# Spreading the node half of a third score pass: even batches stay, odd batches run beside the first and the fourth convolution

## What is computed

```python
def _sage_layer(h, edge_src, edge_dst, W, b):
    msg_sum = segment_sum(h[edge_src], edge_dst, num_segments=n)
    deg = segment_sum(ones_like(edge_dst), edge_dst, num_segments=n)
    m = msg_sum / maximum(deg, 1.0)[:, None]
    return relu(concatenate([h, m], axis=1) @ W + b)
...
x = _layernorm(x + _L0_gnn_ref(...))
x = _layernorm(x + _L1_gnn_ref(...))
x = _layernorm(x + _L2_gnn_ref(...))
x = _layernorm(x + _L3_gnn_ref(x, src, dst, W1, b1, W2, b2))
```

## Time and profile before

| | us |
|---|---|
| median of 3 runs | 5108.9 (5107.18 to 5110.88) |
| the profiled execution, its own time | 5106.98 |
| its span, first to last instruction | 5105.2 |
| busy: TensorE 3933.3, DVE 3846.9, ACT 3417.5, POOL 3021.6 | 77%, 75%, 67%, 59% |
| mean granted TensorE clock | 0.906 |

### The profile page before, as it was taken

The page is one execution under the profiler, slowest core; times in us unless marked ns, Lnnn a source line. Parts: engine busy times, 40 slices in busy tenths (PEclk is TensorE's granted clock), DMA queues, the critical chain, the costliest instruction groups (busy, mean ns, idle before and its releaser), DMA issues. The chain is left out here.

```text
span 5105.2 us, 107944 instructions
## 1 busy us (share of the span) xinstructions
PE 3933.3 (77%) x23968; PEld 2888.5 (57%) x23968; DVE 3846.9 (75%) x14905; ACT 3417.5 (67%) x11259; POOL 3021.6 (59%) x2914
## 2 busy tenths in 40 slices
PE   2999999565996798994998995897767676665554
PEld 1666766343775454773555774443666566665544
DVE  4999999676998787887886998898548777444443
ACT  0889999554886576884776885887448788333332
POOL 2888888475552122661223551787767676777777
PEclk9999999788998899997999997998889888997666
DMA  2566666587996576994777994775546566543332
GB/s 61 164 185 197 200 197 192 169 287 245 353 352 235 185 243 200 346 352 146 237 240 237 352 348 174 228 225 173 157 148 208 186 206 191 156 148 116 92 100 70
DMA packets 605098, 1059.41 MB, mean 208 GB/s; under 512 B 109304, under 2 KB 129930, under 8 KB 604924
## 3 DMA queue, kind: packets, MB, share of 16 engines
q1 hardware_dynamic: 523196, 919.04, 52.7%
q0 software_dynamic: 81728, 138.51, 10.7%
HBM read 607.70 MB, written 453.39 MB: 208 GB/s over the span
## 5 line engine op out<-in xcount | busy, mean ns | idle before, releaser
L2403 POOL DMA_INDIRECT got_c<-table,src_row x980 | 932.1, 951 | 373.1 <-issue 295.0
L1399 POOL DMA_INDIRECT src_got_s<-table,src_row x588 | 554.9, 944 | 474.2 <-PE bank L1445 139.8
L2431 PE MATMUL bank<-pick_c,got_c 128*128 128x128 f32 x1960 | 349.4, 334 | 425.3 <-DMA got_c<-table,src_row 355.6
L1997 PE MATMUL bank<-w_all,dt_m 128*128 128x512 f32 x1176 | 568.1, 599 | 35.3 <-DMA dt_m<-delta_t 33.7
L2431 PEld LDWEIGHTS bank<-pick_c,got_c 128*128 128x128 f32 x1960 | 300.9, 235 | 470.7 <-issue 292.1
L1971 POOL TENSOR_TENSOR part_m<-part_m,half_sum_m 128x512 f32<-128x512 f32 x98 | 158.7, 1619 | 586.0 <-DVE half_sum_m L2204 586.0
L1554 ACT ACTIVATE z_s<-z_s,shift_s,dev_s 128x128 f32<-128x128 f32 x1176 | 483.8, 486 | 1.4 <-DVE shift_s L1673 0.9
L2534 ACT COPY agg_c<-bank 128x512 f32<-128x512 f32 x245 | 143.0, 583 | 450.0 <-DVE bank L1835 298.3
L789 PEld LDWEIGHTS bank<-w_mean,ht 128*128 128x128 f32 x2352 | 313.2, 194 | 143.4 <-issue 143.4
L2455 PE MATMUL bank<-w_c,agg_c 128*128 128x128 f32 x1960 | 377.9, 321 | 2.3 <-ACT agg_c L2534 2.2
L1828 DVE COPY tails_c<-tails_c 128x1 f32<-128x1 f32 x245 | 37.0, 151 | 424.9 <-PE bank L2431 419.6
(11 more groups left out here) (331 smaller groups left out, 11840.9 us busy)
## 6 DMA issues: line engine op xcount, KB each, us to landing
table<-rows SPq DMA_DIRECT2D x294, 256.0 KB
x_s<-table SPq DMA_DIRECT2D x294, 256.0 KB
x_c<-table SPq DMA_DIRECT2D x245, 256.0 KB
table<-mid_s SPq DMA_DIRECT2D x196, 256.0 KB
table<-z_s SPq DMA_DIRECT2D x196, 256.0 KB
table<-z_c SPq DMA_DIRECT2D x196, 256.0 KB
own_rows_s<-table SPq DMA_DIRECT2D x147, 256.0 KB
pick_t_s<-picks_t SPq DMA_DIRECT2D x147, 256.0 KB
```

The source lines that it names most:

```text
L1399: nc.gpsimd.indirect_dma_start(out=src_got[r][:, g, :], out_offset=None, in_=tables[l].rows, in_offset=bass.IndirectOffsetOnAxis(ap=src_ro ...
L1997: nc.tensor.matmul(b_h[k % n_h][:, :], dt[b.slot][:, k, :], w_all[:, l, :, :].rearrange("p h d -> p (h d)"), start=True, stop=True).then_i ...
L2403: nc.gpsimd.indirect_dma_start(out=got[r][:, g, :], out_offset=None, in_=t_in.rows, in_offset=bass.IndirectOffsetOnAxis(ap=src_row[:, t:t ...
L2431: ins = nc.tensor.matmul(b_sum[r][:, k * P:(k + 1) * P], got[b.slot][:, k, :], pick[r][:, k, :], start=k == 0, stop=sage, skip_group_check ...
```

## The change

The third score pass is called with a new flag, `solo`. Then a step treats one edge batch and only node batch `2b`. Its lists are new (`step_solo`), and with one node batch a step the two banks and the paired tiles alternate by step. The 49 odd node batches go to `convolve(0, ...)` and `convolve(3, ...)`, 25 to each (one is done twice): every second step of these phases starts one node batch (`even(b)`). Its tiles are few: one bank `b_turn` for all three uses (turned rows, hidden rows, hidden rows turned back), one bank `b_node` for the second product, and one `nxt` and one `nht`. The waits of the new functions are those that these tiles call for. Each of the two phases also loads the node weights and biases by four more transfers at its start, and TensorE waits for them. Their loops run longer at the end, by up to seven counts on ACT.

```diff
+                        def step_solo(at):        # TensorE, third pass
+                            b = at(1)
+                            if b:
+                                hidden(b, 0)
+                            b = at(2)
+                            if b:
+                                turn_delta(b)
+                                product(b, 0)
+                                turn_hidden(b, 0)
+                            b = at(3)
+                            if b:
+                                score(b)
+                            b = at(0)
+                            if b:
+                                turn_rows(b, 0)
+                            b = at(1)
+                            if b:
+                                spread(b)
...
+                        def step_solo(at):        # ACT, third pass
+                            b = at(1)
+                            if b:
+                                relu(b, 0)
+                            b = at(3)
+                            if b:
+                                deviation(b, 0)
+                            b = at(2)
+                            if b:
+                                delta_out(b)
+                            b = at(3)
+                            if b:
+                                normalise(b, 0)
+                            b = at(0)
+                            if b:
+                                turn_out(b, 0)
+                            b = at(3)
+                            if b:
+                                score_out(b)
...
+                        def step_solo(at):        # DVE, third pass
+                            b = at(3)
+                            if b:
+                                scale(b, 0)
+                            b = at(2)
+                            if b:
+                                residual(b, 0)
+                                middle(b, 0)
+                                moments(b, 0)
+                            b = at(1)
+                            if b:
+                                set_bias(b, 0)
+                                difference(b)
...
+                def even(b):                      # the convolutions
+                    return nodes and b and b.slot % 2 == 0
...
+                        def load_nodes(b):        # SP
+                            r = b.slot // 2
+                            hold(sp, nz_read, b.ring(1, -2))
...
+                        def node_turn(b):         # TensorE
+                            pe.wait_ge(nx_in[r], b.ring4(16))
+                            hold(pe, nmid_made, b.ring(1, -1))
+                            for g in range(GB):
+                                ins = nc.tensor.transpose(b_turn[:, g * P:(g + 1) * P], nx[r][:, g, :], ident[:, :])
+                            ins.then_inc(n_turned, 1)
+                        def node_hidden(b):
+                            pe.wait_ge(nxt_made, b.ring(1))
+                            nc.tensor.matmul(b_turn[:, :], nw1[:, :], nxt[:, :], start=True, stop=True).then_inc(nh_made, 1)
+                        def node_middle(b):
+                            pe.wait_ge(nht_made, b.ring(1))
+                            for g in range(GB):
+                                ins = nc.tensor.transpose(b_turn[:, g * P:(g + 1) * P], nht[:, g, :], ident[:, :])
+                            ins.then_inc(nmid_turned, 1)
+                        def node_product(b):
+                            pe.wait_ge(n_bias, b.ring(1))
+                            for g in range(GB):
+                                ins = nc.tensor.matmul(b_node[:, g * D:(g + 1) * D], nht[:, g, :], nw2[:, :],
+                                                       start=False, stop=True, skip_group_check=True)
+                            ins.then_inc(ny_made, 1)
+                        def node_steps(at):
+                            b = at(4)
+                            if even(b):
+                                node_middle(b)
+                            b = at(5)
+                            if even(b):
+                                node_product(b)
+                            b = at(3)
+                            if even(b):
+                                node_hidden(b)
                         def step_gcn_relu(at):
                             b = at(1)
                             if b:
                                 sum_edges(b)
+                            node_steps(at)
                             b = at(2)
                             if b:
                                 product(b)
+                            if even(b):
+                                node_turn(b)
                             b = at(1)
                             if b:
                                 add_own(b)
...
                             b = at(2)             # step_sage_relu
                             if b:
                                 product(b)
+                            node_steps(at)
+                            b = at(2)
+                            if even(b):
+                                node_turn(b)
...
+                        def node_turned(b):       # ACT
+                            act.wait_ge(n_turned, b.ring(1))
+                            nc.scalar.copy(nxt[:, :], b_turn[:, :]).then_inc(nxt_made, 1)
+                        def node_relu(b):
+                            act.wait_ge(nh_made, b.ring(1))
+                            hold(act, ny_made, b.ring(1, -1))
+                            nc.scalar.activation(flat(nht), b_turn[:, :], ACT.Relu, bias=nb1[:, 0:1]).then_inc(nht_made, 1)
+                        def node_middle_out(b):
+                            act.wait_ge(nmid_turned, b.ring(1))
+                            hold(act, nmid_stored[r], b.ring4(16, -16))
+                            nc.scalar.copy(flat(nmid[r]), b_turn[:, :]).then_inc(nmid_made, 1)
+                            hold(act, nz_read, b.ring(1, -1))
+                            nc.scalar.copy(b_node[:, :], nb2[:, :]).then_inc(n_bias, 1)
...
+                        def node_steps(at):
+                            b = at(3)
+                            if even(b):
+                                node_relu(b)
+                            b = at(4)
+                            if even(b):
+                                node_middle_out(b)
+                            b = at(6)
+                            if even(b):
+                                node_deviation(b)
+                            b = at(7)
+                            if even(b):
+                                node_normalise(b)
                         def step_relu(at):
                             b = at(0)
                             if b and not sage:
                                 diagonals(b)
-                            b = at(2 if sage else 1)
-                            if b:
+                            b = at(2)
+                            if b and sage:
                                 set_bias(b)
                                 sums_out(b)
+                            node_steps(at)
+                            b = at(1)
+                            if b and not sage:
+                                set_bias(b)
+                                sums_out(b)
+                            b = at(2)
+                            if even(b):
+                                node_turned(b)
...
-        edge_scores(2, (io["L3_gnn_W1"][0:D, :], io["c_L3_gnn_b1"]), (io["L3_gnn_W2"][0:D, :], io["b_L3_gnn_b2"]), t[6], t[7], t[8])
+        edge_scores(2, (io["L3_gnn_W1"][0:D, :], io["c_L3_gnn_b1"]), (io["L3_gnn_W2"][0:D, :], io["b_L3_gnn_b2"]), t[6], t[7], t[8], True)
```

More of the change, by code:

```diff
@@ L1216, in _, with edge_scores @@
                         skewed(dve, nb, 2, step, 4)
-        def edge_scores(l, first, second, t_in, t_mid, t_out):
+        def edge_scores(l, first, second, t_in, t_mid, t_out, solo=False):
             with ExitStack() as c, Semaphores(nc) as sem:
@@ L1232, in edge_scores @@
                 scores = pairs("scores", (P, P))
-                x, z = ([fours(f"{n}{h}_") for h in range(2)] for n in ("x", "z"))
+                halves = range(1 if solo else 2)
+                x, z = ([fours(f"{n}{h}_") for h in halves] for n in ("x", "z"))
                 xt = pairs("xt")
@@ L2387, in step @@
                                 store(b)
-                        skewed(sp, nb, 6 if norm else 4, step, 4)
+                            b = at(6)
+                            if even(b):
+                                store_node_middle(b)
+                            b = at(9)
+                            if even(b):
+                                store_nodes(b)
+                        skewed(sp, nb, 9 if nodes else 6 if norm else 4, step, 4)
+                        if nodes:
+                            for r in range(2):
+                                sp.wait_ge(nmid_stored[r], 16 * ((n_own + 1 - r) // 2))
```

(22 more changed lines are left out.)

200 lines of the change are left out of this document (147 added, 53 removed).

## The result

The changed kernel takes 5132.93 us (median of five runs), the kernel before 5108.65 us beside it: a ratio of 1.0045, 95% interval 1.0034 to 1.0057, so 0.45% slower. The forecast was 5130 us. One of the five executions, at 7644.67 us, belongs to a slower state and is left out of the ratio; the other four have a median of 5130.8 us. The profiled execution spans 5126.7 us.

What follows compares the result with a forecast made beforehand. The third pass was full on all engines and transfers; POOL's gathers bound the first and fourth convolution. -96 + 14 + 104 = +22 on 5106.98 gives 5129, with 2 for the median 5130 us; range 5104 to 5176 (8 in 10).

Steps and rivals of the forecast that it cites:

- Third pass, -96: Third score pass: one node batch less a step, 5.5 us in place of 7.52, 49 steps; bounds -98 and -76.
- the loop: Third pass: DVE's list, then TensorE's turn_delta and product, in a chain of 5.44 us a step.
- (b): Third pass: the transfers set the pace, step 5.9 us, 5150 us in all; chance 0.12.
- Fourth convolution, +104: Fourth convolution: TensorE and ACT take turns, 6.9 us a step in place of 5.0; bounds 88 and 118.
- +12: Fourth convolution's end: the last node batch follows the last product alone, about 13 us against 1 now.
- +3: Fourth convolution's start: TensorE waits for four more transfers and fills one more bank; bounds 0 and 5 us.
- +83 and +6: Fourth convolution's steps: 44 steps pay 1.9 us each (+83); the five before have 12.3 us for two (+6).
- First convolution, +14: First convolution: POOL still sets the pace, rate 0; tail +12 and start +2; bounds 10 and 35 us.
- +2: First convolution's start: the addition there was put at 2 us.
- released half a step and more ahead of need: SP's queue: its waits, for a result's store and the load held by the residual, end early; no time added.
- (a): Fourth convolution: the node work hides there too, 5042 us in all; chance 0.10.
- (c): Fourth and first convolution: pauses lower TensorE's clock, +31 and +20 us, 5181 us together; chance 0.12.

Runs made afterwards that it cites:

- the two reorderings: Changed kernel, fourth convolution alone: node steps ahead of the product on TensorE (5632.54 us), or normalisation ahead of the relu on ACT (5682.49 us); changed kernel there 5718.13 us.

## Why the prediction was right

**Third pass, -96.** Measured -95.8, at 5.49 us a step against 5.44 for the loop, 5.2 for the transfers and 5.5 as taken. The waits and the steps of 5.41 us speak for the loop, and the DMA share of 0.99 for the transfers; both are within 0.3 us of the step. The number was right, and which of the two sets it is open: with 0.6 us taken out of the loop on other chips, 0.1 to 0.2 us a step was gained. Rival (b), 5.9 us a step, fell.

**Fourth convolution, +104.** Measured +104.1, and its parts are close. The pair of steps took 13.64 us where 13.8 was summed. The last product ends 19.4 us ahead of the next phase (4599.1 to 4618.55) where it ended 4.1 ahead (4593.4 to 4597.48), so the tail costs +15.4 and not +12. Part of that is the lower clock: over 4598 to 4618 us the granted clock is 0.59, and the eight matmuls of a node product take 1.91 us in place of 1.06. From the start of the phase to the first product it is some 14 us in both kernels, so the start costs nothing, not +3. That these two misses cancel is luck. What is left, 104.1 - 15.4 = 88.7, is the loop, for which the terms +83 and +6 stood. That the order is the cause, and not the amount of work, is shown by the two reorderings, on other chips but with the same cost of the phase (103.8 us): -84 and -37 us at equal work. The second is one item of the chain, 34 us by its row, and it comes within 3 us.

**First convolution, +14.** Measured +13.2. POOL kept its 1.25 us a gather. The last product ends 15.9 us ahead of the next phase (3716.6 to 3732.48) in place of 4.4: +11.5 for the tail. The first product comes 15.2 us after the start of the phase in place of 13.7: +1.6 for the start, put at +2. The runs with one batch less took 8.9 us off the tail on another chip.

**A step that failed without a price.** The prediction held that the node load is "released half a step and more ahead of need". The waits of the changed kernel for 3550 to 3700 us say otherwise:

```profile
PEld bank L2599 <- DMA nx_c<-table: 22.7, 15, 1.7
PE bank L2599 <- DMA nx_c<-table: 19.8, 15, 1.5
```

TensorE waits 1.3 us for it in every pair of steps. POOL's 10.0 us a pair hid this in the first convolution, ACT's chain hid it in the fourth, and it came out when that chain was cut.

**The rivals.** (a), that the node work hides in the fourth convolution, fell on the order of the lists; with `node_hidden` ahead most of it does hide. (c), the clock, fell too: TensorE waits 3.3 us for the sums in each pair of steps (0.84 and 2.46 in the timeline), and the granted clock in that stretch is 1.00. In the first convolution it rose from 0.86 to 1.00, with TensorE's busy share up from 73% to 85%. On a slower chip the fourth convolution of the changed kernel has 0.88 (the window above), and there a product waited up to 3.8 us. The length of the pauses alone doesn't tell the level: in the kernel before, in the first convolution (3600 to 3750 us), the longest wait of TensorE is 2.2 us and the clock 0.86. The Trainium skill (TensorE: Matmul & The Clock Gate, HAM oscillation) describes a kernel in which waits of some 3 to 5 us for transfers bring the clock down before each burst. The pauses in this fourth convolution are shorter than those, so the trace neither bears that out nor speaks against it, and the prediction went too far where it called (c) the likeliest by that page.

## What to carry to other kernels

Work that fits into the idle time of every engine can still make a phase 40% longer (257.6 to 361.7 us here), because lists in fixed order make the engines take turns: write down who waits for whom through two full steps, and place what another engine needs soon ahead of what nobody waits for. Where such work must be added, put what produces for the other engine ahead of the operation that waits for that engine, as `node_hidden` ahead of `product`. The last piece of work whose stages are spread over several steps costs its whole latency behind the loop, here 11.5 and 15.4 us, so start none in the last step.

## What the runs showed that was not expected

Four other chips ran the kernel before in 5610 to 5666 us (medians), 10 to 11% over the 5109 us of the first, at a mean clock of 0.859 in the profiled one rather than 0.906. The time isn't lost evenly. The attention phase after the first score pass takes 339.2 to 339.4 us on both kinds of chip (340 after the second), but the second convolution takes 328.1 in place of 262.3. A POOL gather takes 947 ns, the same.

What differs is idle time inside runs of instructions that wait for nothing. In the kernel before, the sixteen matmuls of a `product` in the sage form need no signal once the first has started. On the first chip the second of each pair (L2458) never idled. On the other, the view of that line (784 of them) says

```profile
L2458 PE MATMUL bank<-w_c,own_c x784: 269/275/580, 4677.7 to 5582.7; 128*128 128x128 f32 x196
its engine sat idle before it (us, times) until:
  issue: 153.6, 172
```

and the timeline of the kernel before on that chip shows one such product, 5.4 us from its first matmul to the next matmuls (4810.82) where the earlier trace rows has 1.89:

```profile
4805.43 0.49 PE L2455 MATMUL bank<-w_c,agg_c 128*128 128x128 f32 x2 [1.16 <-issue]
...
4806.90 0.37 PE L2458 MATMUL bank<-w_c,own_c 128*128 128x128 f32 x1 [0.42 <-issue]
...
4808.31 0.27 PE L2458 MATMUL bank<-w_c,own_c 128*128 128x128 f32 x1 [0.71 <-issue]
...
4810.43 0.59 PE L2458 MATMUL bank<-w_c,own_c 128*128 128x128 f32 x2 [1.62 <-issue]
```

The engine had nothing to wait for by semaphore and stood still for 0.4 to 1.6 us at a time. ACT shows the same (a copy of the sums at 4800.2 us came 3.98 us late, put down to issue). Late instructions would look like this, but no run tested that; the page's instruction queues have the same packets on both chips (54 and 120, a share of 0.1% each), and the cause stays open. The effect on the verdict is large: on such chips the changed kernel is 2.0% slower (1.0175 to 1.0226) rather than 0.45%, mostly since the third pass gives back 37 us in place of 96 and the first convolution costs 32 in place of 13.
